# A transformer block on one core: the last twelve heads run batch by batch, and batch 0 is routed to its experts while batch 1's heads run

## The reference

```python
x = x + layernorm(attention(layernorm(x)))      # x: 2 batches x 1024 tokens x 128
x = x + layernorm(moe(layernorm(x)))

def attention(x, Wq, Wk, Wv, Wo, bo, rel_pos_bias):       # 16 heads of 64
    logits = einsum('bhqd,bhkd->bhqk', q, k)
    logits = (logits + causal + pos_bias(rel_pos_bias)) / 64
    return (softmax(logits) @ v) @ Wo + bo

def moe(x):                                                # 8 experts, hidden size 512
    shared = gelu(x @ Wfc_s + bfc_s) @ Wproj_s + bproj_s
    probs = softmax(x @ Wr)
    topk_p, topk_i = top_k(probs, 2); topk_p /= sum(topk_p)
    return shared + sum over the 2 picked e of (gelu(x @ Wfc[e] + bfc[e]) @ Wproj[e] + bproj[e]) * topk_p
```

## Time and profile before

| | us |
|---|---|
| median of 3 runs (793.38 to 796.9) | 795.07 |
| the profiled execution | 791.7 |
| its span, first to last instruction | 790.0 |
| PE busy | 692.7 (88%) |
| DVE busy | 625.8 (79%) |
| ACT busy | 551.8 (70%) |
| POOL busy | 336.0 (43%) |

### The profile page before, as it was taken

How to read it: one execution, slowest core, us unless ns; L and a number is a source line. 1 busy time by engine, 2 the same in 40 slices (tenths; PEclk the granted TensorE clock), 3 DMA queues, 4 the chain that set the end, 5 groups by cost and what they waited for, 6 DMA issues and landing times.

```text
span 790.0 us, 17201 instructions
## 1 busy us (share of the span) xinstructions
PE 692.7 (88%) x4466; PEld 611.2 (77%) x4466; DVE 625.8 (79%) x1663; ACT 551.8 (70%) x1305; POOL 336.0 (43%) x417
## 2 busy tenths in 40 slices
PE   4977999999999999999999999999966457899930
PEld 4856888888888888888888889888865345899920
DVE  5665888889888898888888888888888616788836
ACT  2355888788888888888887888888824314787823
POOL 2548644243433434334333343342353770155543
PEclk9998999999999999999999999999997768999985
DMA  8693643546436465364553644546200247599723
GB/s 296 244 299 71 167 130 85 150 89 167 129 74 163 87 156 137 71 159 100 143 137 83 160 111 118 137 93 161 88 2 1 80 131 224 197 349 367 268 82 112
DMA packets 82050, 114.85 MB, mean 145 GB/s; under 512 B 42496, under 2 KB 59392, under 8 KB 79584
## 3 DMA queue, kind: packets, MB, share of 16 engines
q1 hardware_dynamic: 79232, 108.71, 49.8%
q0 software_dynamic: 2496, 5.15, 1.8%
q10 hardware_dynamic: 288, 0.59, 0.3%
HBM read 48.32 MB, written 32.56 MB: 102 GB/s over the span
## 4 chain that ended last, share of the span: by engine, by line
PE 72%; DVE 8%; issue 6%; another core or an unknown queue 4%; DMA 3%; ACT 3%; POOL 3%; SPq 1%; ACTq 0%; DVEq 0%; POOLq 0%
PE out_ps L1513 17%; PE score_ps L1480 16%; PE trans_ps L1495 16%; PE shared_ps L1527 7%; PE shared_ps L1388 2%; DVE pT_lo L1335 2%; PE shared_ps L1390 2%; PE shared_ps L1389 2%; PE score_ps L1390 2%; PE score_ps L1388 2%; PE score_ps L1389 2%; DVE stats L1016 1%; PE trans_ps L1388 1%; POOL y_scratch L746 1%
## 5 line engine op out<-in xcount | busy, mean ns | idle before, releaser
L832 ACT ACTIVATE probs<-score_ps,row_min 128x128 f32<-128x128 f32 (+7 forms) x256 | 190.1, 743 | 54.4 <-DVE row_min L1088 54.0
L853 ACT ACTIVATE pT_hi<-trans_ps 128x512 fp32r<-128x512 f32 (+3 forms) x384 | 185.3, 492 | 45.7 <-PE trans_ps L1495 34.1
L1101 DVE TENSOR_TENSOR pT_lo<-trans_ps,pT_hi 128x512 fp32r<-128x512 f32 (+3 forms) x384 | 201.7, 552 | 17.8 <-ACT pT_hi L853 17.6
L1088 DVE CUSTOM_DVE_ANT_0 score_ps<-score_ps,bias 128x128 f32<-128x128 f32 (+7 forms) x256 | 194.6, 760 | 26.6 <-PE score_ps L1480 23.3
L1495 PE MATMUL trans_ps<-ident,probs 128*128 128x128 f32 x1152 | 191.1, 275 | 3.2 <-DVE pT_lo L1101 1.8
L1480 PE MATMUL score_ps<-k_hl,q_hl 128*128 128x512 f32 (+2 forms) x768 | 182.9, 352 | 7.2 <-DMA k_hl<-k_hl 5.6
L640 POOL TENSOR_TENSOR acc<-acc,head_out 128x512 f32<-128x512 f32 x64 | 82.8, 1294 | 222.0 <-DVE head_out L1121 221.9
L1495 PEld LDWEIGHTS trans_ps<-ident,probs 128*128 128x128 f32 x1152 | 137.6, 141 | 27.5 <-DVE pT_lo L1101 11.9
L1513 PE MATMUL out_ps<-pT_hi,v_hl 128*128 128x512 f32 (+2 forms) x384 | 156.8, 409 | 1.1 <-DVE pT_lo L1101 1.1
L1480 PEld LDWEIGHTS score_ps<-k_hl,q_hl 128*128 128x128 f32 x768 | 134.9, 189 | 27.7 <-DMA k_hl<-k_hl 5.8
L1513 PE MATMUL out_ps<-pT_lo,v_hl 128*128 128x512 f32 (+2 forms) x384 | 133.3, 347 | 0.0
(11 more groups left out here) (252 smaller groups left out, 1168.3 us busy)
## 6 DMA issues: line engine op xcount, KB each, us to landing
q_hl<-k_hl SPq DMA_DIRECT2D x64, 256.0 KB, 3.7
k_hl<-k_hl SPq DMA_DIRECT2D x32, 512.0 KB, 4.4
v_raw<-v_scratch SPq DMA_DIRECT2D x32, 256.0 KB, 4.6
split_scratch<-normed_rows SPq DMA_DIRECT2D x16, 512.0 KB, 5.3
k_hl<-split_scratch SPq DMA_DIRECT2D x16, 512.0 KB
rows_scratch<-wv SPq DMA_DIRECT2D x16, 455.0 KB, 6.6
v_scratch<-probs SPq DMA_DIRECT2D x12, 512.0 KB, 5.1
normed_rows<-in_W_halves SPq DMA_DIRECT2D x16, 256.0 KB, 4.2
```

What stands on the lines that cost most here:

```text
L832: act.activation(probs[s % 4][:, 0:n], scores_of(s % QB)[:, 0:n], ACT.Exp, bias=row_min[:, s:s + 1], scale=-1.0, accum_out=row_sum[:, s:s ...
L853: act.activation(pT_hi[c][:, CH * g:CH * g + m, q * P:(q + 1) * P], trans_ps[k % 2][:, 0:m * P].rearrange("p (m q) -> p m q", q=P), ACT.Co ...
L1088: dve.tensor_tensor_reduce(out=ps, in0=ps, in1=bias_b[b][:, T - n:T], scale=1.0, scalar=3e38, op0=ALU.add, op1=ALU.min, accum_out=row_min[ ...
L1101: dve.tensor_tensor(pT_lo[c][dst], trans_ps[k % 2][:, 0:m * P].rearrange("p (m q) -> p m q", q=P), pT_hi[c][dst], ALU.subtract).then_inc(p ...
```

## The change

1. `LAST = 12`: heads 0 to 3 still run both batches. The next six passes (program heads 4 to 9) run real heads 4 to 15 of batch 0, two per pass, and passes 10 to 15 the same heads of batch 1. `unit(h, b)` says which. q's and k's weights are split once more per pass. The loop is heads 1 and 2 only; 3 to 15 are straight code.
2. `route_early(z)` on each engine: z counts the 96 slots of passes 10 to 15. In them batch 0, whose attention is complete, gets its norms, logits, choice, ranks and slots piece by piece, and 13 of its 16 scatters in slots 88 to 95; the other 3 come before the last additions to acc. Its scaled addition of acc into x is done by POOL in two tensor_tensor per chunk.
3. Behind the heads batch 1 is one group, with the norms in chunks of four blocks. Logit matmuls have 16 columns. PE and ACT run the first part of the shared layer before batch 1's transposes and norm.
4. The shared layer's weights are split in heads like the experts' (18 halves, two each in heads 5 and 6) and loaded by DMA.
5. Token p*16+t instead of t*128+p stands in partition p of block t, in the numbers given to POOL and in the loads at the end; pieces of these are 2 KB instead of 512 B, and of a tile's rows 1040 B instead of 520 B.

```diff
+    LAST = 12
+    F = H - LAST
+    P0 = F + LAST // B
+    TWICE = (F + 1, F + 2)
+    NORM_SLOTS = [41, 42, 43, 44, 46, 47, 48, 49]
+    SCATTERS = {88: 2, 89: 2, 91: 2, 92: 2, 93: 2, 94: 2, 95: 1}
+    EARLY = sum(SCATTERS.values()) - QB
+    PICKS = [(0, QB), (QB, NB)]
+    def unit(h, b):
+        if isinstance(h, int) and h >= F:
+            i = B * (h - F) + b
+            return F + i % LAST, i // LAST
+        return h, b
+    def early_slot(h, s):
+        return B * QB * (h - P0) + s if isinstance(h, int) and h >= P0 else -1
...
-                                 y_dram[lo:lo + W, :].rearrange("(t p) d -> p t d", p=P)).then_inc(y_loaded[c], 16)
+                    src = bass.AP(y_dram.tensor, (k * B * T + CH * c) * D, [[NB * D, P], [D, CH], [1, D]])
```

POOL, called at the end of each slot, and what follows the last head:

```diff
+            def route_early(z):
+                if z in (16, 22):
+                    lo = CH * (z == 22)
+                    root(1, lo, lo + CH)
+                if z in (21, 27):
+                    add_residual(int(z == 27))
+                if z in (33, 39):
+                    lo = CH * (z == 39)
+                    root(2, lo, lo + CH)
+                if z == 40:
+                    name_rows(0)
+                if z == 56:
+                    pool.wait_ge(moe_in_ready, QB)
+                    pool.tensor_copy(rows[1][0][:, :, 0:D], rows[0][0][:, :, 0:D]).then_inc(rows_copied, 1)
+                for n in range(SCATTERS.get(z, 0)):
+                    k = sum(m for y, m in SCATTERS.items() if y < z) + n
+                    dispatch(0, k // QB, k % QB)
...
-            dispatch(0)
-            dispatch(1)
+            for t in range(EARLY, QB):
+                dispatch(0, 1, t)
...
+            for g in range(1, len(PICKS)):
+                for i in range(2):
+                    for t in range(*PICKS[g]):
+                        dispatch(g, i, t)
```

DVE:

```diff
+            def route_early(z):
+                if z == 9:
+                    dve.wait_ge(acc_added, P0 * B * NC)
+                if 9 <= z < 21:
+                    moments_in_pieces(acc, CH * ((z - 9) // 6), (z - 9) % 6)
+                if z in (23, 25):
+                    lo = CH * (z == 25)
+                    stand(lo, lo + CH).then_inc(std_ready, 1)
+                if z in (29, 35):
+                    dve.wait_ge(residual_added, 1 + (z == 35))
+                if 29 <= z < 41:
+                    moments_in_pieces(x_sb, CH * ((z - 29) // 6), (z - 29) % 6)
+                if z in (37, 43):
+                    lo = CH * (z == 43)
+                    scale_and_offset(2, lo, lo + CH)
+                if z in (53, 61):
+                    nT_evac(1, int(z == 61))
+                if z in (69, 71):
+                    take_logits(0, int(z == 71))
+                if 74 <= z < 78:
+                    choose(0, (z - 74) // 2, (z - 74) % 2)
+                if z in (78, 79):
+                    share(0, int(z == 79))
+                if 85 <= z < 88:
+                    find_slots(0, z - 85)
```

PE, and what follows its last head:

```diff
+            def route_early(z, h, s, last):
+                if z in (52, 60):
+                    wait_shared(h, s, last)
+                    transposes(1, int(z == 60))
+                if z in (54, 62):
+                    pe.wait_ge(nT_ready, NCH + 1 + (z == 62))
+                if z == 68:
+                    wait_shared(h, s, last)
+                    logits(0)
+                if z == 70:
+                    pe.wait_ge(logit_taken, 1)
+                if z == 84:
+                    wait_shared(h, s, last)
+                    ranks(0)
+                if z == 86:
+                    pe.wait_ge(ranks_taken, 1)
...
-            keep_busy(56)
-            for c in range(NC):
-                transposes(1, c)
-            pe.wait_ge(wo_scaled, H * B * NC)
-            pe.wait_ge(nT_ready, NCH + NC)
-            logits(0)
-            pe.wait_ge(wfc_ready, 1)
+            pe.wait_ge(shared_w_loaded, 32)
             hidden_units(0, 0, 0)
-            keep_busy(16, trans_ps[0])
-            ranks(0)
-            for c in range(NC, NCH):
-                transposes(1, c)
+            hidden_units(0, 1, 0)
+            keep_busy(32, trans_ps[1])
+            transposes(1, NC)
+            transposes(1, NC + 1)
             pe.wait_ge(nT_ready, 2 * NCH)
             logits(1)
+            keep_busy(16, trans_ps[0])
             ranks(1)
-            hidden_units(0, 1, 0)
             second_layer(0, 0, 0)
```

606 lines of the change are left out of this document (341 added, 265 removed).

## The result

The change makes the kernel slower by 0.7%: 799.31 us (median of 11 runs, 798.41 to 804.06) against 793.38 for the kernel before on the same chip (11 runs), ratio 1.0073, 95% interval 1.0045 to 1.0100. The forecast was 773. The profiled execution has a span of 796.8 us where it was 790.0, 6.8 more.

| station | before | after | difference | new in this stretch |
|---|---|---|---|---|
| head 10's first row minimum (DVE) | 377.6 | 378.6 | +1.0 | +1.0 |
| head 15's first row minimum | 540.0 | 561.8 | +21.8 | +20.8 |
| head 15's last row minimum | 569.8 | 594.5 | +24.7 | +2.9 |
| last add into acc ends | 586.8 | 616.7 | +29.9 | +5.2 |
| last slot numbers | 622.0 | 641.8 | +19.9 | -10.0 |

What follows compares the result with a forecast made beforehand. PE bounds the heads; behind them no engine is full, and scatters accompany a slow stretch. First tile -19.1 us (including +5.5 in the heads) and final loads -2 make -21.1 from 791.7: 770.6 profiled, 773 as median, range 762 to 788.

Steps and rivals of the forecast that it cites:

- D = +5.5 us at the heads' end, range 0 to 17: Heads 10 to 15: batch 0's early routing adds 4.6 us on PE and 0.9 for DVE and waits.
- POOL's +1: Behind the last head: POOL, late from the early scatters, delays the last add into acc by 1 us, or 0.
- That fits on average: Heads 10 to 15: DVE's 17.7 us of added routing work fits a slack of 22.8 us, except in head 14.
- most like L1238, 0.22 each: Heads 10 to 15: some 50 added DVE instructions at about 0.22 us each, 11.0 us in all.
- rival C: Last head: scatters slower beside a busy DVE, at most 0.26 us each, 3.4 us later; total 776, chance 0.09.
- The routing behind the heads: From acc's last add to batch 1's slots: one batch only, slots 10 us sooner with POOL's 1 us counted.
- no load of the activation table costs there: Routing behind the heads: added table loads, 1.28 us each, are hidden and cost nothing, or +1.3 if one isn't.
- The slow stretch: Table to first tile: 26 us undisturbed plus 6 lost while scatters slow the engines, range of the loss 0 to 13.
- rival D: Scatters beside dense work slow all engines: last head +13 us, acc 3, behind the routing 7 more; total 797, chance 0.12.
- Rival A: Behind the heads: 16 scatters never start the slow stretch; 6 us less, total 767, chance 0.22.
- Rival B: Heads 12 to 15: DVE bounds them, delaying the next slot's row minimum and PE; 15 us, total 782, chance 0.12.
- Part 4: End of the kernel: loading y in pieces of 2 KB saves 2 us, between -3 and 0.

Runs made afterwards that it cites:

- experiment 5: experiment 4's kernel with the routing's pieces moved out of slots where POOL adds and some waits set further apart: 789.7 us, ratio 0.9996 to the kernel before.
- experiment 6: Kernel before plus idle DVE instructions; per head: 13 two-input additions away from POOL 33.18 us, three beside it 35.80, three reductions there 32.71, three additions behind each scaling 37.57.
- experiment 2: Kernel before plus idle work, one kind per head: 16 matmuls of 16 columns 34.75 us, a PE-ACT-DVE round trip 34.24, eight ACT activations 32.71.
- experiment 3: Changed kernel without the 32 early DVE statistics and aggregates in heads 10 to 12: 797.07 us, ratio 1.0091 to the kernel before.
- experiment 4: Changed kernel with all 16 of batch 0's scatters moved behind the heads, ahead of batch 1's: 799.57 us, ratio 1.0125 to the kernel before.
- experiment 1: Kernel before plus idle DVE instructions; per head: 16 spread reductions 33.22 us, eight 32.80, sixteen in one place 34.43, 16 two-input additions 35.94.
- experiment 10: Kernel before with a POOL copy of 128x512 behind every second of the 32 scatters: 787.51 us, ratio 0.9961.

## Why the prediction was wrong, step by step

**The step that failed is D, "D = +5.5 us at the heads' end, range 0 to 17".** It measured 24.7 us at the last row minimum, and 29.9 at the last add with the tail in it, for which the forecast had POOL's +1. What the runs put in its place: 7.0 us of DVE instructions held by POOL's (timeline after; experiments 5 and 6), where nothing was forecast; two round trips of 1.55, 3.1 us (experiment 2; forecast 1.3 for their transposes); the logits' matmuls 2.05 (experiment 2; forecast 2.2); 1.1 to 1.7 for the statistics (experiment 3; forecast 0); 7.2 for the scatters (experiment 4; forecast 1 as POOL's lateness). That is 20.5 to 21.1 of 29.9. Straight code adds some 0.2 us a head (32.7 in the undisturbed ones of experiment 2, 32.5 in the loop), 2.4 us over heads 3 to 14. The rest, 6 to 7 us, I can't divide: moving the pieces won 8.5 us in heads 10 to 14 against experiment 4, where the lumps are 5.2 of the 7.0, so part of it may be waits between pieces that stood too close.

Within the step two arguments failed. "That fits on average" took 3.8 us of slack per head for usable. For pieces of 0.2 us it nearly is (experiment 1: 0.6 us for 3.3), but a single hold-up of 1 us or more costs nearly its whole length (experiments 1 and 6). The likely reason is that the row minimum, the exponential, the transposes and the split hang together from slot to slot. And every duration was read from rows in which nothing collided: "most like L1238, 0.22 each". The trace of before had the warning, in a row of DVE's timeline beside POOL's addition at 580.71, which I read past:

```profile
580.77 1.23 DVE L1027 TENSOR_TENSOR newton<-rstd 128x8 f32<-128x8 f32 x1 [0.90 <-POOL rstd L591]
```

An instruction on 8 columns that lasts 1.23 us beside an addition of 1.26 is one that waits. The same section of the Trainium skill that the prediction cited against rival C ("SBUF — State Buffer", section "SBUF: two separate sides") states the other half of the rule too: of a DVE instruction with two inputs in SBUF and a GpSimd instruction that reads SBUF, the one that starts first holds back the other for its whole length. Experiment 6 agrees, 0.22 against 1.27 us. I took from the Trainium skill the half that concerns scatters (0.96 us in the heads after as before) and left the half that concerned the change.

**The routing behind the heads was right**: from acc to slots 25.1 us where 35.1 had been, 10.0 less, where the forecast has 11 for this stretch alone. That no load of the activation table costs there was right: behind exp's, 1.28 us at 631.10, ACT still waits 3.18 us for the logits, and gelu's at 635.83 runs while DVE chooses.

**The slow stretch was sized nearly right and its nature left open.** From table to first tile 33.1 us, forecast 26 + 6 = 32. But I let it act behind the heads alone, and rival D, which put it beside the last head, was right in part: experiment 4 gives 7.2 us for it there, D had 13 + 3. D's reason, that dense work brings it on at once, fell: head 15's last row minimum comes at the same time with seven scatters ahead of it as with none (594.50 and 594.41), and the stretch begins with about as many scatters gone as behind the heads before. The rate decides: ten to twelve scatters at 1.27 us apiece begin it (in the last head with one pause of 5 us among them), and 1.65 us apiece doesn't (experiment 10). Whether anything fills up meanwhile, and what, stays open; what the trace shows is work that ends, or is reported, late (7.8 us behind its record in experiment 4). Rival A, that sixteen never begin it, was wrong.

**Rival B** (pieces in single slots make the next row minimum late and PE waits) had the place right and 15 us for it; it held each piece to 0.7 us at most, named no cause for a longer one, and was given 0.12. **Rival C** was wrong: the scatters in the heads are 0.95 to 1.25 us each, 1.27 apart.

**Part 4** brought nothing where -2 was forecast. The sentence from the Trainium skill ("DMA: Bandwidth & Descriptors", section "Specifications"), line rate from 512 B on, agreed with the trace as to time: higher slices at the end, the same 8 us. From the first tile to the end it is 118.5 us for 118.3.

The sum with the measured terms: 29.9 - 10.0 - 13.2 = +6.7, and 6.8 in the span.

## What to carry to other kernels

Before work goes into an engine's slack, list what the neighbours run in just those slots: a short DVE instruction with two SBUF inputs that comes behind the instruction which releases POOL will meet POOL's, and a slot without POOL beside it takes the same instruction almost for free (13 of them cost 0.5 us in experiment 6). Slack in a pipeline whose stages hand over every 2 us takes work in pieces of 0.2 us and gives next to nothing for a piece of 1 us or a round trip. Where engines wait for something unnamed beside a burst of indirect DMAs, try a slower burst before moving it.

## What the runs showed of the hardware

A DVE instruction on 128x64 with two SBUF inputs took 0.21 us alone and 1.27 to 1.32 when it started just behind a POOL tensor_tensor on 128x512 (1.27); a reduction at the same place stayed at 0.21. A DVE cast of 128x8 took 0.96 us for 0.17 beside POOL (580.57), so it isn't the second input alone. An addition of 128x64 that began 0.16 us ahead of POOL's stayed at 0.22 (580.07). Indirect scatters of 128 rows every 1.27 us left PE busy 45% of the time (625 to 656 before) after about twelve, with waits up to 12.3 us that no engine's work explains; at 1.65 us apiece they didn't. The medians moved with it (790.65 to 787.51). Whether the recording of the profile takes part in it isn't shown: every run on record has a span and a granted clock, so none is known to be without it.
